# A decoder layer in three stages: the second stage's first work moved into the first stage's last steps, and the order at the second stage's end changed

## What is computed

```python
x = layernorm(x + attn(x, ...))          # gated mix of linear attention and window attention
x = layernorm(x + xattn(x, ctx, ctx))    # softmax cross attention, 16 heads of 16
x = layernorm(x + ffn(x, ...))           # 32 experts, 4 chosen for each token, and a shared expert
# attn:  h = layernorm(x); lin, win = linear(h), window(h)
#        gate = sigmoid(relu([lin, win, h] @ wg1 + bg1) @ wg2 + bg2)
#        out = (gate * lin + (1 - gate) * win) @ wo + bo + x
# xattn: q, k, v = x @ Wq.T, ctx @ Wk.T, ctx @ Wv.T;  softmax(q k / 4) v @ Wo.T
# ffn:   sum over the 4 experts of w * (silu(x @ gate) * (x @ up)) @ down, plus the same of the shared expert
```

## Time and profile before

| What | us |
|---|---|
| median of 3 executions | 744.39 (743.49 to 745.38) |
| the profiled execution, its own time | 745.36 |
| its span, first to last instruction | 743.6 |
| PE busy | 614.5 (83%) |
| DVE busy | 536.7 (72%) |
| ACT busy | 535.1 (72%) |
| POOL busy | 518.5 (70%) |
| first second-stage instruction of ACT | 264.85 |
| PE's first product of the second stage | 269.74 |
| first gather of the third stage issued | 550.65 |

### The profile page before, as it was taken

The page is one execution under the profiler, slowest core; times in us unless marked ns, Lnnn a source line. Parts: engine busy times, 40 slices in busy tenths (PEclk is TensorE's granted clock), DMA queues, the critical chain, the costliest instruction groups (busy, mean ns, idle before and its releaser), DMA issues. The chain is left out here.

```text
span 743.6 us, 23938 instructions
## 1 busy us (share of the span) xinstructions
PE 614.5 (83%) x7764; PEld 515.9 (69%) x7764; DVE 536.7 (72%) x2065; ACT 535.1 (72%) x1555; POOL 518.5 (70%) x671
## 2 busy tenths in 40 slices
PE   2899999999999548878778878878659999999384
PEld 1678988988887437667666666677548878878162
DVE  3988989988886226788889889767825766676374
ACT  4889999999998239997899898857116766666122
POOL 4758999999989943654888877657602766676574
PEclk9999999999999858998999889778778999999798
DMA  8310000000000012232454453423784556563294
GB/s 300 106 39 2 3 2 4 2 15 22 3 3 2 2 51 78 73 108 89 127 177 131 126 181 123 136 79 123 203 199 124 155 143 190 178 189 103 84 354 148
DMA packets 57081, 77.65 MB, mean 104 GB/s; under 512 B 8440, under 2 KB 46464, under 8 KB 56832
## 3 DMA queue, kind: packets, MB, share of 16 engines
q1 hardware_dynamic: 44480, 54.78, 25.1%
q0 software_dynamic: 7632, 16.87, 6.5%
q10 hardware_dynamic: 4848, 4.47, 1.9%
HBM read 44.39 MB, written 27.36 MB: 97 GB/s over the span
## 5 line engine op out<-in xcount | busy, mean ns | idle before, releaser
L1881 POOL DMA_INDIRECT y_rows<-yo,ix x95 | 93.6, 985 | 66.8 <-DVE ix L1977 39.2
L517 ACT ACTIVATE sc<-sc,mn 128x128 f32<-128x128 f32 x256 | 82.6, 416 | 2.4 <-DVE mn L679 2.4
L1216 POOL DMA_INDIRECT x_rows<-rows,slot_ix x64 | 64.0, 1001 | 22.1 <-issue 17.3
L1906 ACT ACTIVATE gT<-bank 128x512 f16<-128x512 f16 x95 | 56.1, 595 | 31.8 <-DVE eh_lo L1981 13.8
L1285 ACT ACTIVATE scx<-bank,mnx 128x128 f32<-128x128 f32 x256 | 74.4, 442 | 4.4 <-DVE mnx L1379 4.1
L1187 POOL TENSOR_TENSOR we_lo<-east,we_hi 128x256 f16<-128x256 f32 (+1 forms) x80 | 59.5, 770 | 11.5 <-ACT we_hi L1259 11.3
L679 DVE CUSTOM_DVE_ANT_0 sc<-bank,rel 128x128 f32<-128x128 f32 x256 | 57.5, 286 | 0.8 <-issue 0.5
L1385 DVE TENSOR_TENSOR pTx_lo<-bank,pTx_hi 128x512 f16<-128x512 f32 x64 | 43.7, 682 | 10.6 <-ACT pTx_hi L1293 10.5
L1648 PE MATMUL bank<-ident,scx 128*128 128x128 f32 x256 | 46.3, 310 | 3.0 <-ACT scx L1285 2.5
L688 DVE TENSOR_TENSOR pT_lo<-bank,pT_hi 128x512 f16<-128x512 f32 x64 | 43.2, 676 | 6.7 <-ACT pT_hi L524 6.6
L1973 DVE COPY yo<-bank 128x256 f32<-128x256 f32 x63 | 26.7, 424 | 25.9 <-PE bank L2089 24.2
(11 more groups left out here) (308 smaller groups left out, 2545.0 us busy)
## 6 DMA issues: line engine op xcount, KB each, us to landing
east<-in_experts SPq DMA_DIRECT2D x32, 384.0 KB, 3.5
hT<-x_rows SPq DMA_DIRECT2D x95, 129.0 KB
rows<-xhl SPq DMA_DIRECT2D x16, 512.0 KB, 4.5
hT<-y_rows SPq DMA_DIRECT2D x16, 512.0 KB, 5.6
x_rows<-padrow SPq DMA_DIRECT2D x21, 129.0 KB, 6.4
wst<-in_wcat SPq DMA_DIRECT2D x8, 256.0 KB, 6.5
cst<-in_ctx_t SPq DMA_DIRECT2D x16, 128.0 KB, 3.3
out<-fin ACTq DMA_DIRECT2D x16, 128.0 KB, 4.4
```

Of the source, the lines that this page charges most:

```text
L517: done = act.activation(sc[:, g, j], sc[:, g, j], ACT.Exp, bias=mn[:, n % 2, g, j:j + 1], scale=-1.0)
L1216: pool.indirect_dma_start(shared.x_rows, bass.IndirectOffsetOnAxis(ap=slot_ix[:, n, k:k + 1], axis=0), rows4[:, q, k], None).then_inc(shar ...
L1881: pool.indirect_dma_start(c.y_rows, bass.IndirectOffsetOnAxis(ap=ix[:, n % IX], axis=0), yo[:, n % YO], None, bounds_check=NDEST - 1, oob_ ...
L1906: act.activation(gT[:, n % U], GT_BANK[n % len(GT_BANK)], ACT.Copy).then_inc(gt_r, 1)
```

## The change

**Front.** Tiles 0 and 1 of the second stage get their q, k and v projections with all their halves inside the first stage's last steps, and tile 2 gets its x1 halves, transposes and copy: x1_high, c_high (ACT), x1_low, c_low (now DVE), x1_T, q_proj, k_proj, v_proj (PE), x1T_, xq_high, xk_high, xv_high (ACT), xq_low, xk_low, xv_low (DVE), in steps 20 to 22. The second stage's helpers skip these tiles. The two context loads, the five small loads, the f16 identity and three of POOL's seven memsets move into the first stage too, with their buffers and semaphores; later buffers (shid, sh_hi, sh_lo, yo, eg) are laid over the same memory.

**End.** sh_out moves behind sh_in(n, 1) and weighted, to the end of PE's step; sh_add behind sh_low; the tables from DVE's step 20 to behind its loop; ACT's 12 paddings into its step 23, six on each side of sh_gate(5, 1). SP's gather into slot n waits only for the sh_in products that read the memory under that slot. PE waits for the last sh_add only where it first writes that bank (tile 2 of the third stage).

```diff
+FRONT, FRONT_X = 2, 3
...
+                    for n in range(FRONT):
+                        sp.dma_start(cst[:, n], ctx_tiles[:, :, n]).then_inc(ctx_in[n], 16)
+                    sp.dma_start(tri[:], consts[:, P:2 * P]).then_inc(rc_in, 16)
+                    sp.dma_start(known[:], consts[:, 2 * P + NE:2 * P + 2 * NE + 1]).then_inc(k_in, 16)
+                    sp.dma_start(first[:], consts[:, 2 * P:2 * P + NE]).then_inc(rc_in, 16)
+                    sp.dma_start(dest_f[:].rearrange("p n k -> p (n k)"), consts[:, 2 * P + 2 * NE + 1:]).then_inc(rc_in, 16)
+                    sp.dma_start(rbias[:], rbias_d.rearrange("(a n) -> a n", a=1).broadcast_to([P, NE])).then_inc(rc_in, 16)
...
-                    for i in range(NB + 6):
+                    for i in range(NB + 7):
+                        if i == NB + 4:
+                            act.activation(ident16[:], ident[:], ACT.Copy).then_inc(id16_r, 1)
+                            for n in range(FRONT):
+                                x1_high(n)
+                                c_high(n)
...
+                        if i == NB + 5:
+                            xq_high(0)
+                            xk_high(0)
+                            x1T_(1)
                         gt_(i - 6)
+                        if i == NB + 4:
+                            x1T_(0)
+                            xv_high(0)
+                        if i == NB + 5:
+                            xv_high(1)
+                        if i == NB + 6:
+                            xq_high(1)
+                            xk_high(1)
+                            x1_high(2)
+                            x1T_(2)
                         pT_high(i - 4, 2)
                         exps(i - 3, 0)
...
+                    def x1_low(n):
+                        dve.wait_ge(x1hi_r, n + 1)
+                        dve.tensor_tensor(x1[:, n % 2, 1], xs[:, n], x1[:, n % 2, 0], ALU.subtract).then_inc(x1lo_r, 1)
+
+                    def c_low(n):
+                        dve.wait_ge(chi_r, n + 1)
+                        dve.tensor_tensor(c_lo[:, n], cst[:, n], c_hi[:, n], ALU.subtract).then_inc(clo_r, 1)
+
...
                         st2(i - 8)
+                        if i == NB + 4:
+                            for n in range(FRONT):
+                                x1_low(n)
+                                c_low(n)
+                        if i == NB + 5:
+                            xv_low(0)
+                            xq_low(0)
+                            xk_low(0)
+                        if i == NB + 6:
+                            xv_low(1)
+                            xq_low(1)
+                            xk_low(1)
+                            x1_low(2)
...
+                    def v_proj(n):
+                        pe.wait_ge(emptied["NUM"], NB)
+                        wait(pe, front_emptied["XPV"], n)
+                        pe.wait_ge(clo_r, n + 1)
+                        pe.wait_ge(w_lo_late, len(W_PIECES) - NPROJ)
+                        front_products("XPV", lambda s, k, m: C[s][:, n, k], lambda s, k, m: W[s][:, k, C_XV:C_XV + D], 1, D)
...
                         branches_T(i - 5)
+                        if i == NB + 5:
+                            q_proj(0)
+                            k_proj(0)
+                            x1_T(1)
                         out_proj(i - 7)
+                        if i == NB + 5:
+                            v_proj(1)
+                        if i == NB + 6:
+                            x1_T(2)
...
                         transposed(i - 4, 3)
+                        if i == NB + 4:
+                            x1_T(0)
                         gate1(i - 5)
+                        if i == NB + 4:
+                            v_proj(0)
+                        if i == NB + 5:
+                            q_proj(1)
+                            k_proj(1)
                         numerator(i - 4)
...
-                layer.on_sync(sp, lambda: sp.wait_ge(filled["GU1"], NCH))
+                layer.on_sync(sp, lambda batch: sp.wait_ge(filled["GU1"], min(batch, NB - 1) // 2 + 1))
...
+                    if i == PADS_AT:
+                        pad_rows(act, mybir.EngineType.Activation, PADS_SP, (PADS_SP + NE) // 2)
                     sh_gate(i - FIRST_SH - 1, 1)
-                    if i >= NB + 7:
-                        e = PADS_SP + (i - NB - 7) * (NE - PADS_SP) // 4
-                        pad_rows(act, mybir.EngineType.Activation, e, e + (NE - PADS_SP) // 4)
+                    if i == PADS_AT:
+                        pad_rows(act, mybir.EngineType.Activation, (PADS_SP + NE) // 2, NE)
...
                     xv_low(i - 1)
-                    sh_add(i - FIRST_SH)
                     mins(i - 1, 1)
                     weights(i - 5)
                     places(i - 5)
...
                         dve.tensor_scalar(shared.fill_row[:], shared.count[:], -1.0, None, ALU.add).then_inc(shared.fill_r, 1)
                     mins(i - 1, 0)
                     sh_low(i - FIRST_SH + 1)
+                    sh_add(i - FIRST_SH)
                     scores_(i - 4)
...
-                    if i == NB + 4:
-                        layer.tables(dve)
+                layer.tables(dve)
                 layer.on_vector(dve)
...
                     k_proj(i - 2)
-                    sh_out(i - FIRST_SH - 1)
                     transposed(i - 3, 2)
                     q_proj(i - 1)
                     sh_in(i - FIRST_SH, 1)
                     weighted(i - 3, 0)
-                for u in ("CN", "LG", "GU0", "GU1", "SD"):
-                    pe.wait_ge(emptied[u], {"CN": NB // 2, "LG": NB, "GU0": 2 * NCH, "GU1": 2 * NCH, "SD": NCH}[u])
+                    sh_out(i - FIRST_SH - 1)
+                for u in ("CN", "LG", "GU0", "GU1"):
+                    pe.wait_ge(emptied[u], {"CN": NB // 2, "LG": NB, "GU0": 2 * NCH, "GU1": 2 * NCH}[u])
                 pe.wait_ge(xpv_rd, NB)
-                layer.on_tensor(pe)
...
+            if n < G:
+                read_up_to((4 * RW * (n + 1) - 1) // (2 * 2 * KT * P))
             if by_expert(n - G):
                 sp.wait_ge(yo_r, n - G + 1)
...
+                if n < len(GT_BANK):
+                    shared_done(banks[5 + n])
```

More of the change, by code:

```diff
@@ L35 @@
 PADS_SP = 20
+PADS_AT = NB + 7
 ROUTE_SCALE = 2.5
@@ L139, in decoder_kernel, with in_front @@
         padrow = sb("padrow", [P, RW], U32)
+        tri, ones, ident16 = sb("tri", [P, P]), sb("ones", [P, P]), sb("ident16", [P, P], F16)
+        rbias, first, known = sb("rbias", [P, NE]), sb("first", [P, NE]), sb("known", [P, 1 + NE])
+        dest_f = sb("dest_f", [P, NB, TOPK])
+        front = sb("front", [P, FRONT_WORDS], F16)
+        f_at = [0]
+        def in_front(words):
+            f_at[0] += words
+            assert f_at[0] <= FRONT_WORDS
+            return front[:, f_at[0] - words:f_at[0]]
+        x1 = in_front(4 * D).rearrange("p (b s d) -> p b s d", b=2, s=2)
+        x1T = in_front(4 * D).rearrange("p (b s k t) -> p b s k t", b=2, s=2, k=KT)
+        cst = in_front(4 * D).bitcast(F32).rearrange("p (b k t) -> p b k t", b=2, k=KT)
+        c_hi, c_lo, xq_hi, xq_lo = (in_front(2 * D).rearrange("p (b k t) -> p b k t", b=2, k=KT) for _ in range(4))
+        xk_hi, xk_lo = (in_front(4 * D).rearrange("p (b k h t) -> p b k h t", b=2, k=KT, h=2) for _ in range(2))
+        xv_hi, xv_lo = (in_front(2 * NH * (HD + 1)).rearrange("p (b h d) -> p b h d", b=2, h=NH) for _ in range(2))
         x_rows = nc.dram_tensor("x_rows", ((NE * BLOCKS + 1) * P, RW), U32, kind="Internal").ap()
@@ L733, in st2, with xq_low, xk_low, xv_low @@
                             dve.bn_aggr(mv2[:, s], stats2[:, s]).then_inc(ln2_mv, 1)
+                    def x1_low(n):
[4 more added lines that the diff above has]
+                        dve.tensor_tensor(c_lo[:, n], cst[:, n], c_hi[:, n], ALU.subtract).then_inc(clo_r, 1)
+                    def xq_low(n):
+                        dve.wait_ge(xqhi_r, n + 1)
+                        dve.scalar_tensor_tensor(xq_lo[:, n], front_room["XPQ"][:, 0:D].rearrange("p (k t) -> p k t", k=KT), -QK_SCALE, xq_hi[:, n],
+                                                 ALU.mult, ALU.subtract).then_inc(front_emptied["XPQ"], 1)
+                    def xk_low(n):
+                        dve.wait_ge(xkhi_r, 2 * (n + 1))
+                        for b in range(2):
+                            dve.scalar_tensor_tensor(xk_lo[:, n, :, b], front_room["XPK"][:, 0:D].rearrange("p (k t) -> p k t", k=KT), par[:, b:b + 1],
+                                                     xk_hi[:, n, :, b], ALU.mult, ALU.subtract).then_inc(front_emptied["XPK"], 1)
+                    def xv_low(n):
+                        dve.wait_ge(xvhi_r, n + 1)
+                        dve.wait_ge(front_set, 3)
+                        dve.tensor_tensor(xv_lo[:, n, :, 0:HD], front_room["XPV"][:, 0:D].rearrange("p (h d) -> p h d", h=NH), xv_hi[:, n, :, 0:HD],
```

(27 more changed lines are left out.)

144 lines of the change are left out of this document (87 added, 57 removed).

## The result

The changed kernel takes 739.65 us in the median of seven executions (736.17 to 742.37), the kernel before 745.38 on the same chip (743.49 to 746.03). The ratio is 0.9938, with a 95% interval of 0.9912 to 0.9965: 4.6 us faster, where 10.8 were forecast. The profiled execution took 736.17 us, 9.2 less than that of before. It is the quickest of the seven. So there are two questions: which of the forecast's terms held, and why the profiled execution gained twice what the medians did.

What follows compares the result with a forecast made beforehand. No engine was taken as full throughout, so the seams between stages were read as the bound. Tail +4.6, head −9.5 and end −5.9 sum to −10.8 us: 733.6 from 744.39; own range 729 to 738, 8-in-10 range 728.5 to 740.5.

Steps and rivals of the forecast that it cites:

- Tail of the first stage: First stage's last steps: the work put into them loses 4.6 us in three places, bounds 1.5 to 8.
- (a): First stage's tail, step 20: four low parts on DVE contend with POOL; 2.0 us lost, bounds 0.1 to 2.6.
- (b): First stage's tail: v_proj(0) behind gate1(15), and xv_high(0) ahead of z1f(15); 1.2 us lost, bounds 0.9 to 1.7.
- (c): First stage's tail: yt(14), which gate2(15) awaits, stands behind tile 0's low parts; 1.4 us lost, 1.0 to 3.5.
- Head of the second stage: Second stage's start: exponentials 5.4 us behind the barrier, tile 0's step 1.0 shorter; 9.5 us gained, bounds 7 to 11.5.
- End of the second stage: Second stage's end: spreading product at 555.5 instead of 561.74; 5.9 us gained, bounds 2 to 9.
- ACT held "some 9.5 us": Second stage's end: ACT's two blocks of six paddings and two register loads take some 9.5 us, until about 536.6.
- "The tables now stand behind that [...] Both meet.": Second stage's end: tables behind the last sh_add end at 555.1, meeting PE's gathered tiles ready at 555 to 556.
- rival 2: Second stage's end doesn't move: paddings land late, gathers, tables and PE as late as before; 739.0, chance 0.13.
- Rival 4: Second stage's end: ACT's padding issues back up at saturated DMA, making it slower; 748 at 2.0 us each, chance 0.05.
- Rivals 1 and 3: 1: first-stage tail stretches by everything added, 738.5, chance 0.15; 3: experts' stream paces second stage, 743.1, chance 0.06.
- One sign: Second stage: distance from first exponentials to the spreading product becomes 276.1 us, from 283.04 before.

Runs made afterwards that it cites:

- no_front: Kernel before plus constants' loads early and the end's edits, tables left in step 20, no front work in the first stage: ratio 0.9898 to the kernel before.
- tables_back3: Changed kernel with the tables back in step 20 of DVE's loop, run on the long chip: ratio 0.9909 to the kernel before.
- look_a: Changed kernel unchanged, run for one more profiled execution on a quick chip; no median or ratio of its own given.
- look_b: Changed kernel unchanged, another profiled execution on the same chip; no median or ratio of its own given.
- look_c: Changed kernel unchanged, another profiled execution on the same chip; middle 2.1 us from the first profile's; no median or ratio given.
- one_load: Changed kernel with tables in step 20 and ACT's padding registers loaded once instead of twice: ratio 0.9877 to the kernel before.
- tables_back2: Changed kernel with the tables back in step 20 of DVE's loop, on the quick chip: 734.17 us, ratio 0.9868 to the kernel before.
- pads_sp: Changed kernel with tables in step 20 and all 32 paddings issued by SP, none by ACT: ratio 0.9909 to the kernel before.
- consts_early: Kernel before with only the five loads of the second stage's constants, and their buffers, moved into the first stage: ratio 0.9962.

## Why the prediction was wrong

**Tail of the first stage: right.** 5.25 us for 4.6, and by its places: (a) 2.24 for 2.0, with three of DVE's four low parts at 0.89 to 0.95 and one at 0.42 (all four in 3.0 us; the forecast's "up to 4.2 us" can't be redone from its rows); (b) 0.8 for 1.2; (c) 1.2 for 1.4; 1.0 more up to the barrier, for which the forecast had nothing. Place (a) rested on sharing: DVE's 0.42 grew to 0.95 beside a busy POOL. The rule named there (the Trainium skill, "SBUF — State Buffer", "Who interferes with whom") agrees with these durations.

**Head of the second stage: right in size, wrong in what earned it.** Exponentials 5.07 us behind the barrier for 5.4; tile 0's step to the next shorter by 1.2 (8.81 us for 10.01), forecast 1.0. Tail and head together are −5.0 at tile 1 in the means of the table above, forecast −4.9. But constants early alone gave 4.3 of it, with the tail's last gt (255.62 for 255.51) where it was before. The forecast wrote "PE's wait for constants is gone within this" and never priced it alone; so the front work's own net was not seen. It is 0.7 us at tile 1 on the quick chip and 2.2 in the one pair on the long chip (no_front against tables_back3), and on the whole time it doesn't show.

**End of the second stage: the step that failed.** 5.9 us were forecast; over the executions of the table above the end is 80.0 before and 79.8 after. By the forecast's own mark, the spreading product, it gained 1.2 (71.4 us behind tile 15 for 72.6), and gave 1.0 back between it and the first store (8.4 for 7.3), where the forecast had 0.3 for a colder PE. Two terms of the step:

1. *ACT held "some 9.5 us".* It was 13.2, and 14.0 to 15.0 in look_a, look_b and look_c. The second load of registers took 3.3 us in the changed kernel (525.63 to 528.96), where the forecast took 1.09 from the earlier trace rows; one_load, without it, had ACT free 3.1 us sooner. The paddings took 0.78 and 0.61 each. So sh_high(5) came 13.6 us behind sh_gate instead of 9.6, and the end of the last sh_add gained 2.9 against tile 15 (66.0 for 68.9 in the means) instead of 8.3.
2. *"The tables now stand behind that [...] Both meet."* Taking the tables out of step 20 was counted as a gain of the shared chain. There was next to none: ACT's hold begins at the same place and is longer, so DVE waits in any case, and with the tables back in step 20 it still has 7.6 us to spare. Moved behind the last sh_add, the tables are bare, and PE waits 3.73 us for them. tables_back2 shows both: the chain's end is less than 1 us later (66.8 for 66.0) and the end of the stage 3.9 us earlier. Two delays that lie side by side were priced one behind the other.

The time of rival 2 (739.0, "the end doesn't move") is what came, but not by its mechanism: the first gather was issued at 539.29, 58.6 us behind tile 15, where before it was 62.1. Paddings and scatters were not what the end waited for; the tables were. Rival 4's mechanism, paddings that hold ACT longer, was there in part: 13.2 us, not the 20 that would have eaten the gain. Rivals 1 and 3 are excluded by the first seam: the tail grew by 5.25 us and not by 9.5, and the exponentials did come earlier.

One sign came out right by luck. The forecast wanted 276.1 us from the first exponentials to the spreading product; the first profile has 276.87 (552.04 less 275.17). But the other three profiles of the changed kernel have 277.4 to 279.8, and of the 6.2 us that the first one gained there 1.9 came ahead of tile 1's pTx_hi, 2.4 in the middle and 1.9 at the end, where the forecast had 1.0, nothing and 5.9.

**The middle: the condition that the forecast set itself.** It said that it would be wrong "if the second stage's steps in the middle change by more than some 2 us", for which no row spoke. They changed: 194.6 us in the mean of four for 197.3 in the mean of three. That is 2.7 of the 8.4 us by which the profiled executions differ (737.3 for 745.7 in the mean), and no work was removed there: PE does 2114 to 2116 products in the middle in all seven, at a mean granted clock of 0.88 or 0.89. In the two steps shown above, what differs between executions is the clock that the same products met; the other steps were not traced to it one by one. Whether the new places of sh_out and sh_add in each step bear on the difference between the two kernels is not shown. Against it speak look_c and pads_sp, which have the new order and take the last step in 21.1 and 21.5 us like the kernel before, and consts_early, which has the old order and a middle of 195.4, within the changed kernel's 193.7 to 195.8. Head 5.0, middle 2.7, end 0.2 and 0.3 elsewhere give the 8.2 to 8.4; without the middle some 5.5 remain, which is near the 4.6 to 5.7 of the timed runs.

What stays open: the timed executions leave no trace, so that their middles are as long as before is inferred, not shown. That the profiled gain is twice the timed one may in part be the sample: the three profiled executions of the kernel before took 745.4 to 746.0, its timed ones had a median of 745.38, 744.12 and (one alone) 742.62 on the same chips. Nor is it shown what sets the clock's phase. The Trainium skill, "TensorE: Matmul & The Clock Gate", section "Part 1: The HAM clock gate (the "warmup" mystery)", says that the clock gate judges by a window that runs free of the kernel, so that one kernel runs a different number of matmuls slowly from run to run; the seven middles above, 193.7 to 198.5 us, are in line with it, but don't show what the gate looks at. And on the long chip, where steps 8 to 14 took 14 to 18 us for 12 to 16, there is no profile of the kernel before, and the cause of the longer steps is open.

The best version run is the changed kernel with the tables left in step 20: 0.986 to 0.991 of the kernel before, and below the changed kernel on both chips that had the two, clear of noise on one. With one load of registers it can't be told from that.

## What to carry to other kernels

Before work is taken off an engine's chain, look for what else holds the same consumer at that moment: if another engine is held as long, the work is already hidden, and moving it uncovers it. Price the removal of a plain wait (here five small loads issued one stage late) by itself before anything built around it. And where a stage's steps move with the granted clock, one profiled execution of each kernel can't size a change of under one per cent; profile several, cut them at the seams, and carry over to the median only what repeats.

## What the runs showed of the hardware

A load of six registers from SBUF by ACT took 3.0 to 4.6 us between two blocks of six paddings, and a load of six or twelve took 0.7 to 1.0 ahead of the first block. The DMA engines were fuller in the middle (mean busy share 1.09 in the changed kernel from 525.63 to 528.96 us) than ahead (0.42 from 519.55 to 520.45). Their share alone doesn't explain it: in the kernel before, a load of three took 1.25 us at a share of 1.02 (541.68 to 542.93). A candidate is what ACT itself had just issued; no run tells that apart.

The same ten f32 products took 1.2 us at full clock and 2.2 at half, and the same 24 f16 ones 1.5 and 2.8; which clock they met differed between executions of one kernel on one chip. Between profiled executions of one kernel the middle differed by 2.1 and 2.4 us in some 195, and by 4.4 between pads_sp and the changed kernel, with the same instructions in nearly all of it.
